# Softmax attention with an adaptive temperature: the first pass leads by three units instead of two, and PE's side blocks stand ahead of the next unit's second-pass pieces

## What is computed

```python
def adaptive_temperature_softmax(logits):
    original_probs = jax.nn.softmax(logits, axis=-1)
    entropy = jnp.sum(-original_probs * jnp.log(original_probs + 1e-09), axis=-1, keepdims=True)
    e2 = entropy * entropy
    poly_result = POLY[0] * e2 * e2 + POLY[1] * e2 * entropy + POLY[2] * e2 + POLY[3] * entropy + POLY[4]
    beta = jnp.where(entropy > 0.5, jnp.maximum(poly_result, 1.0), 1.0)
    return jax.nn.softmax(logits * beta, axis=-1)

q, k, v = (proj(Wq), proj(Wk), proj(Wv))       # 16 heads of 8 channels
sim = jnp.einsum('bhid,bhjd->bhij', q, k) / math.sqrt(hd)
sim = jnp.where(causal, neg, sim)
attn = adaptive_temperature_softmax(sim)
out = jnp.einsum('bhij,bhjd->bhid', attn, v)
return out.transpose(0, 2, 1, 3).reshape(b, n, d) @ Wo.T + bo
```

## Time and profile before

| what | value |
|---|---|
| median of three timed runs | 2244.86 us |
| the profiled execution's own time | 2242.96 us |
| its span, first to last instruction | 2241.2 us |
| PE, PEld, DVE, ACT busy over the span | 72%, 31%, 66%, 62% |
| mean granted TensorE clock | 0.758 |
| first-pass evacuations start | 754.1 to 1831.0 us |

### The profile page before, as it was taken

One profiled execution on the slowest core, in us unless ns is written; L12 is line 12 of the kernel. 1 busy time (PEld: TensorE's weight loads), 2 busy tenths in 40 slices (PEclk: granted clock), 3 DMA queues, 4 the chain that ended last, 5 costly groups with the idle time before them and its releaser, 6 DMA issues. The chain is left out here.

```text
span 2241.2 us, 22322 instructions
## 1 busy us (share of the span) xinstructions
PE 1608.5 (72%) x6402; PEld 689.7 (31%) x6402; DVE 1480.7 (66%) x3478; ACT 1393.1 (62%) x2635; POOL 141.7 (6%) x126
## 2 busy tenths in 40 slices
PE   4787899999999643777767778667777787511166
PEld 2443344444444201222222222223222233201144
DVE  6645354535464798887787787877878774479922
ACT  3564443434333697899987999879999997300012
POOL 0000000000000100000000000000000000035365
PEclk9898899999999755676666765666666769755578
DMA  4000065454556201101011010010110103240031
GB/s 146 0 0 0 13 162 156 131 154 132 155 150 171 58 32 39 62 33 62 24 39 60 33 50 34 31 71 26 42 40 28 54 13 98 58 122 0 0 102 49
DMA packets 56667, 147.36 MB, mean 66 GB/s; under 512 B 7760, under 2 KB 22480, under 8 KB 53936
## 3 DMA queue, kind: packets, MB, share of 16 engines
q1 hardware_dynamic: 52320, 136.63, 20.6%
q0 software_dynamic: 3072, 8.39, 1.2%
q10 hardware_dynamic: 1152, 0.92, 0.3%
HBM read 126.38 MB, written 19.53 MB: 65 GB/s over the span
## 5 line engine op out<-in xcount | busy, mean ns | idle before, releaser
L1682 DVE CUSTOM_DVE_ANT_0 sa_lg<-sa_e,sa_lg 128x1024 f32<-128x1024 f32 (+7 forms) x512 | 386.4, 755 | 93.4 <-ACT sa_lg L1573 92.9
L1423 PE MATMUL sa_ps<-sa_space 72*128 72x512 bf16 (+3 forms) x768 | 293.0, 450 | 212.5 <-DVE sa_nmax L1673 148.0
L1563 ACT ACTIVATE sa_e<-sa_e,sa_nmax 128x1024 f32<-128x1024 f32 (+7 forms) x512 | 415.9, 812 | 36.2 <-DVE sa_nmax L1673 36.1
L1673 DVE CUSTOM_DVE_ANT_0 sa_e<-sa_ps,sa_mask 128x1024 f32<-128x1024 f32 (+7 forms) x512 | 385.5, 753 | 71.3 <-PE sa_ps L1423 69.9
L1573 ACT ACTIVATE sa_lg<-sa_e,sa_sum 128x1024 f32<-128x1024 f32 (+7 forms) x512 | 414.9, 810 | 5.1 <-DVE sa_prod L1682 4.6
L1581 ACT ACTIVATE sa_p<-sa_ps 128x512 f32<-128x512 f32 x576 | 345.8, 626 | 40.8 <-PE sa_ps L1475 30.9
L1472 PE MATMUL sa_ps<-sa_q2s,sa_k2s 75*128 75x512 bf16 (+3 forms) x768 | 298.0, 432 | 66.9 <-ACT sa_p L1581 55.2
L974 DVE TENSOR_TENSOR mx_hw<-mx_spread,mx_h 128x512 f32<-128x512 f32 x256 | 176.0, 691 | 232.8 <-PE mx_ps L813 193.3
L875 ACT ACTIVATE mx_h<-mx_ps 128x512 f32<-128x512 f32 (+1 forms) x264 | 157.0, 597 | 277.0 <-PE mx_ps L800 256.4
L800 PE MATMUL mx_ps<-mx_f,m 128*128 128x512 f32 x512 | 262.0, 597 | 0.8 <-ACT mx_h L875 0.8
L813 PE MATMUL mx_ps<-mx_hw,m 128*128 128x512 f32 x512 | 259.9, 594 | 0.6 <-DVE mx_hw L974 0.6
(11 more groups left out here) (322 smaller groups left out, 1864.3 us busy)
## 6 DMA issues: line engine op xcount, KB each, us to landing
mx_spread<-mx_spill SPq DMA_DIRECT2D x256, 256.0 KB, 4.0
sa_space<-sa_spill_q SPq DMA_DIRECT2D x96, 96.0 KB
sa_space<-sa_spill_k SPq DMA_DIRECT2D x96, 96.0 KB
sa_k2s<-sa_spill_k SPq DMA_DIRECT2D x48, 192.0 KB
sa_q2s<-sa_spill_q SPq DMA_DIRECT2D x48, 192.0 KB
m<-m_in SPq DMA_DIRECT2D x1, 4256.0 KB, 18.7
records<-sa_e SPq DMA_DIRECT2D x8, 512.0 KB, 5.2
be_w<-w_in SPq DMA_DIRECT2D x16, 256.0 KB, 12.5
```

The costliest lines, as they stand in the source:

```text
L1423: last = nc.tensor.matmul(out[:, col:col + w], q_ring[:, c % 2, local, i * P:(i + 1) * P], k_ring[:, c % 2, local, col:col + w], start=Tru ...
L1563: nc.scalar.activation(e[:, u % 5, 0:w], e[:, u % 5, 0:w], ACT.Exp, scale=-1.0, bias=nmax[:, b % 2, i, h:h + 1], accum_out=sums[:, b % 2, ...
L1673: nc.vector.tensor_tensor_reduce(out=e[:, u % 5, 0:w], in0=slot_of("unit", u)[:, 0:w], in1=mask_wide[:, SEQ - w:SEQ], scale=1.0, scalar=3. ...
L1682: nc.vector.tensor_tensor_reduce(out=lg[:, u % 2, 0:w], in0=e[:, u % 5, 0:w], in1=lg[:, u % 2, 0:w], scale=1.0, scalar=0.0, op0=ALU.mult, ...
```

## The change

Four things change together.

1. `AHEAD` is 3 instead of 2: at u, PE computes S(u+3) and DVE does E(u+3). ACT's list and DVE's products keep their u. Before the loop three units are scored and evacuated instead of two.
2. On PE the pieces of u+1 and their answers stand behind the side blocks of u instead of ahead of them.
3. All offsets of side blocks rise by one, so that a block still falls between two wide units. The steps of DVE and ACT that read a block move with it; the ones that prepare it (`entropy`, `set_beta`, `split_shift`, the steps of the norm) and the splits of q2 at 8, 9, 10 stay.
4. The order of the slots' users follows from the same tables.

```diff
-AHEAD = 2
+AHEAD = 3
...
-        WIDE_AT, SHIFT_AT = 7, 9
-        A_AT, Q_AT, K_AT, V_AT = 83, 87, 89, 107
-        TURN_AT, ATT_AT, PROJ_AT = 9, 13, 17
+        WIDE_AT, SHIFT_AT = 8, 10
+        A_AT, Q_AT, K_AT, V_AT = 84, 88, 90, 108
+        TURN_AT, ATT_AT, PROJ_AT = 10, 14, 18
...
-            yield from (("unit", 0), ("unit", 1))
+            yield from (("unit", u) for u in range(AHEAD))
...
-                score(0)
-                score(1)
+                for u in range(AHEAD):
+                    score(u)
                 for u in range(END):
                     if u + AHEAD < ALL1:
                         score(u + AHEAD)
-                    for m in pieces2_at(u + 1):
-                        second(m)
-                        if m % GROUP == GROUP - 1 and m >= GROUP:
-                            answer(m // GROUP - 1)
                     if (k := side_at(u, WIDE_AT)) is not None:
                         widen(k)
...
                     if (b := scores_at(u, 18)) is not None:
                         score_experts(b)
+                    for m in pieces2_at(u + 1):
+                        second(m)
+                        if m % GROUP == GROUP - 1 and m >= GROUP:
+                            answer(m // GROUP - 1)
...
-                evacuate(0)
-                evacuate(1)
+                for u in range(AHEAD):
+                    evacuate(u)
```

## The result

The changed kernel is slower. Five runs have a median of 2260.12 us against 2244.95 us of the kernel before on the same chip; the ratio is 1.0066, interval 1.0053 to 1.0079: +15 us where −12.6 was forecast. The profiled execution has a span of 2259.1 us, 17.9 more.

The account below looks back on a forecast made before the run. ACT was taken to set the pace, DVE almost level, with ACT's idle time clustered at side blocks. Terms 8.3 − 5.6 − 12.8 − 2.5 = −12.6 us gave 2232 us, 8-in-10 range 2224 to 2249.

Parts of the forecast that it names:

- the held E: On DVE, E(u+3) waits for Pr(u-2) directly in front: 0.12 us a unit, +8.3 us in sum.
- costs nothing there: Among pieces DVE has idle time beyond the hold's 0.12 us a unit, so the hold costs nothing there.
- The sum ahead of the pieces: Before pieces run: 4.8 us for 66 units, 2.4 for the next 20, about 1.1 at the start; +8.3.
- My upper bound of +17: Upper end for the hold ahead of the pieces, with its 0.12 us a unit doubled.
- rival B: No change: waits only move, the piece behind its block costs as much; about 2243 us, chance 0.19.
- my terms for it: Gains at side blocks: 0.7 us per `widen`/`turn_shift` pair, 6.4 per full cluster (12.8 for two), 2.5 for the first.
- the pairs `widen`/`turn_shift`: Shift blocks on PE, DVE and ACT: X(12) and units behind 0.7 us ahead, 8 × 0.7 = −5.6 us.
- At q and k: Blocks q and k: L(90) starts at 1190.5, not 1193.47; L(93) at 1201.7, not 1205.13; gain 3.4 us.
- I counted the lead as nothing: E one unit sooner on ACT: its wait moves from X on E to L on Pr, nothing saved.
- The signs: Eight units 11.8 to 12.0 us, E waits below 12, Pr above 12, shifts about 20, pieces near 28, last E 12 sooner.
- A: Slower: wide E and wide Pr in one position delay L at 23 side blocks, 22 us; about 2254 us, chance 0.17.
- C: The held E is free: its 8.3 us becomes 1.1, giving 2225 us; chance 0.08.

Follow-up runs that it names:

- the swapped kernel: The changed kernel with E's two waits in the other order, first for Pr(u-2), then for its scores: ratio 1.0003 to the kernel before.
- six buffers: The changed kernel with six buffers e instead of five, so E(u+3) waits for Pr(u-3): 2235.87 us, ratio 0.9951 to the kernel before.
- the order alone: The kernel before with only the pieces of u+1 moved behind the side blocks of u, lead of two and offsets as before: 2246.43 us, ratio 1.0004.
- lead three, six e and three lg: The changed kernel with six buffers e and three lg: 0.9932 with pieces behind the blocks, 0.9931 in front, 0.9930 with E's waits swapped (pieces behind).
- with the pieces in front, six e alone: The changed kernel with six buffers e and the pieces moved back in front of the side blocks: 2234.27 us, ratio 0.9932.

## Why the prediction was wrong

**The step that failed is the held E**, "0.12 us a unit", "Sum +8.3", and with it "costs nothing there". The place was right. The price was read from a plain operation with a single wait. E has two waits, the one for Pr is written second, and that costs 0.227 us; the swapped kernel, with the wait for Pr first, pays 0.118 a unit, which is my 0.12. The price alone is what lies between those two kernels, 1.0066 and 1.0003, 14 us of the miss of 28.

The sum ahead of the pieces held only in its first part. For the 66 units the measured price gives (0.227 − 0.047) × 66 = 11.9 us, and the lag at X(64) is 11.1, with the start in it. For the 20 units after it gives 20 × 0.227 = 4.5, where the lag grows by 0.4 from X(64) to X(80) and shrinks by 1.1 with six buffers: the hold costs 1.5 there. So the terms would sum to 17.5 where the trace has 11.5. The start itself, 1.1 in the forecast, is 0.9 at X(8) with six buffers. My upper bound of +17 was also added up wrongly: (0.24 − 0.047) × 66 + 20 × 0.24 + 1.1 is 18.6. I took the nearest row and kept too little of the far end in the range, which ended at 2249.

**The cover among pieces was not whole.** I wrote that the hold "costs nothing there". It costs 10.4 us from X(76) to X(472). Between the clusters the cover is there, as said. At the clusters it is not, and my account of it, not shown hold by hold, is that DVE is the late engine there. I had reckoned up to 3 us for it only under rival B. Even at the price that I forecast the change would therefore not have gained: the swapped kernel, at 0.118, stands at 1.0003, and from X(76) to X(472) it gains 7.4 us where the six-buffer kernel gains 13.0.

**The blocks.** Without the hold (six e) the stage between the shifts gains 16.1 us, where my terms for it came to 20.2 (7 × 0.7 + 12.8 + 2.5); 2.2 of the 16.1 lie in the last stretch, in which the first pass ends. By the starts of L1595 in that trace and the kernel before's, the stretches of the two later sequences' clusters gave 6.4 and 9.4 us, for 6.4 and a pair's 0.7 each; the first one's none (+0.9, for −2.5 and −0.7); and the pairs `widen`/`turn_shift` none (+0.7, +0.1, +0.3 in the three stretches that hold one alone, for −0.7 each). All of this is one trace of each. For the pair, two waits came out otherwise than laid out. The layout by hand had L(6) 0.8, the piece 0.9, the shifts 2.6; in the kernel with six e ACT's timeline has:

```profile
997.97 0.94 ACT L1573 ACTIVATE sa_lg<-sa_e,sa_sum 128x768 f32<-128x768 f32 x1 [0.76 <-DVE sa_prod L1682]
...
1003.36 0.83 ACT L1573 ACTIVATE sa_lg<-sa_e,sa_sum 128x640 f32<-128x640 f32 x1 [0.83 <-DVE sa_prod L1682]
...
1009.34 0.60 ACT L1581 ACTIVATE sa_p<-sa_ps 128x512 f32<-128x512 f32 x1 [1.01 <-PE sa_ps L1472]
...
1014.59 1.01 ACT L1595 ACTIVATE sa_shift<-sa_ps 24x1024 bf16<-24x1024 bf16 x1 [3.34 <-PE sa_ps L1440]
```

The first, L(4) behind a Pr(2) that follows the steps of the temperatures, was missing; the fourth, the shifts, is 3.34 where I had 2.6. The other two are as forecast. Together 5.94 us against 4.97 before (0.30 [the wait of X(6)], 3.48, 1.19), where the forecast's three came to 4.3.

At q and k the layout was close. The changed kernel's rows, for the earlier trace rows:

```profile
1198.55 1.23 DVE L1737 TENSOR_SCALAR sa_space<-sa_ps 128x1024 f32<-128x1024 f32 x1 [0.20 <-PE sa_ps L1403]
...
1204.73 1.04 ACT L1573 ACTIVATE sa_lg<-sa_e,sa_sum 128x896 f32<-128x896 f32 x1 [2.66 <-DVE sa_prod L1682]
...
1207.09 0.60 ACT L1581 ACTIVATE sa_p<-sa_ps 128x512 f32<-128x512 f32 x1 [1.31 <-PE sa_ps L1475]
...
1211.03 0.60 ACT L1581 ACTIVATE sa_p<-sa_ps 128x512 f32<-128x512 f32 x1 [2.03 <-PE sa_ps L1475]
```

L(90) starts 6.18 us behind the start of the reading of q; I had 6.2. L(93) starts 17.08 behind it (at 1215.63), for my 17.35 and 20.78 before. The piece behind block k waits 1.31 us, not 2.0: the block took 2.78 us there at a granted clock of 0.67, where before it took 3.65 at 0.53, and no term of mine allowed for that.

**What gains.** I counted the lead as nothing and gave the gain to the order. It is the other way round: the order alone gives nothing, the lead without the hold 0.5 to 0.7%. The sentence that ACT's wait moves from E to Pr was right in kind: 33.6 us of waits for E became none, and 33.0 for Pr stand in the changed kernel. Yet the wait begins one X later. By which part of it the gain comes, the X done sooner, the narrow pairs or the offsets that rose with it, was not separated.

**The signs.** Eight units took 12.7 us, not 11.8 to 12.0. The waits for E and for Pr went the way forecast, those for the shifts fell to 25.2 and not 20, those for pieces rose to 38.9, and the last E came 11 us later than 1831, not 12 sooner. Neither sign of being wrong appeared, pieces over 45 us or L's waits growing (by 28.4) more than E's fell (by 33.6): they looked at ACT's waits from 840 us on, and most of the loss came by X(64).

**The rivals.** A had the right side by luck and the wrong cause: in the kernels with six buffers the wide pair is there and no loss. Of B, the part on the order is shown. C fell, and with it the rule it rested on. The Trainium skill's VectorE: DVE Perf Modes, section "The DRAIN you can't avoid", says of chained copies on DVE that a semaphore behind each costs nothing extra. For E behind Pr the measurement differs and decides: 0.12 us as the first of two waits, 0.227 as the second.

The kernels with lead three, six e and three lg are 0.7% below the kernel before and 1.3% below the changed one; with the pieces in front, six e alone measure the same (0.9932).

## What to carry to other kernels

When work is moved ahead in a ring of buffers, count which operation now stands directly in front of the one that takes the buffer: if that is the one that frees it, on the same engine, each turn pays the hold wherever the engine has no idle time to cover it, and one more buffer takes it away. Of an instruction's waits, write first the one that will be met last: in these DVE lists it stands on the instruction itself, and the others in one of their own ahead of it. The reordering here, on an engine off the critical path, turned one wait of the critical engine into another; sum all waits of that engine before and after, not the one that the edit is aimed at. And mark stages by the same unit of work, not by an event that the edit moves.

## What was not expected of the hardware

A DVE instruction with two waits starts 0.038 us behind the event it waited for if that wait is written first (E behind Pr, swapped kernel), and 0.147 behind it if it is written second (changed kernel); for scores of PE the same, 0.04 and 0.15. With a third, long-met wait behind them the second one still costs, 0.13. The wait written second is a separate instruction of DVE's sequencer (L1672), and E starts 0.084 us behind its end. Without a wait on the operation in front, E starts 0.08 us before that operation's accumulator read ends.
